# Wavelet, convolution and median kernel: one more operand of TensorE in rounded parts, x loaded again into z, and a new order of POOL's and ACT's work

## The reference

```
cA,cH,cV,cD = dwt2(x)                     # one Haar level: sums and differences of pixel pairs
proc(c)     = relu(batchnorm(einsum('bchw,oc->bohw', c, conv_w)))   # statistics over the whole batch
rimg0 = idwt2(proc(cA), proc(cH), proc(cV), proc(cD))
rimg1 = three Haar levels down and up again                          # gives x back
y = conv3x3(concat([rimg0, rimg1], channels), convW_w) + convW_b
y = relu(batchnorm(y))                                               # second batch norm
m = median of the 3x3 pixels around each pixel (zeros outside)
out = y + einsum('bchw,oc->bohw', m, L1_W) + L1_b
```

## Time and profile before

| | |
|---|---|
| median of 3 runs | 402.18 us (400.51 to 403.07) |
| profiled execution, its own time | 403.58 us |
| its span | 401.2 us |
| mean granted TensorE clock | 0.991 |
| PE busy | 383.8 us, 96% |
| DVE busy | 372.2 us, 93% |
| POOL busy | 232.5 us, 58% |
| ACT busy | 170.8 us, 43% |

### The profile page before, as it was taken

The page is one execution under the profiler, slowest core; times in us unless marked ns, Lnnn a source line. Parts: engine busy times, 40 slices in busy tenths (PEclk is TensorE's granted clock), DMA queues, the critical chain, the costliest instruction groups (busy, mean ns, idle before and its releaser), DMA issues.

```text
span 401.2 us, 3603 instructions
## 1 busy us (share of the span) xinstructions
PE 383.8 (96%) x1106; PEld 205.1 (51%) x1106; DVE 372.2 (93%) x487; ACT 170.8 (43%) x351; POOL 232.5 (58%) x213
## 2 busy tenths in 40 slices
PE   6889999999999999999999999999999999998776
PEld 2245578866454555555555545454545464443222
DVE  2889967999999999999999999999999999999994
ACT  2456674446252433333334343333424221379661
POOL 3999559460694664738474747465564740016791
PEclk9999999999999999999999999999999999999988
DMA  7980010010101001010101010101011000002665
GB/s 290 418 364 2 2 52 2 0 52 2 53 1 52 17 37 52 0 52 0 54 0 52 1 54 1 52 1 52 8 46 33 19 2 1 0 0 119 247 248 223
DMA packets 7793, 26.69 MB, mean 67 GB/s; under 512 B 992, under 2 KB 1248, under 8 KB 7776
## 3 DMA queue, kind: packets, MB, share of 16 engines
q1 hardware_dynamic: 7776, 26.48, 17.6%
HBM read 18.09 MB, written 8.39 MB: 66 GB/s over the span
## 4 chain that ended last, share of the span: by engine, by line
PE 81%; DVE 12%; POOL 3%; DMA 2%; issue 1%; SPq 0%; ACT 0%; DVEq 0%
PE conv_ps L429 60%; PE conv_ps L444 12%; PE one_ps L411 4%; PE one_ps L530 3%; DVE y L1004 2%; PE conv_ps L554 2%; DMA z<-x 2%; POOL y L241 1%; POOL y L242 1%; DVE one_ps L916 1%; DVE one_ps L925 1%; DVE sorted_cols L876 1%; DVE sorted_cols L923 1%; DVE one_ps L910 1%; DVE sorted_cols L883 1%
## 5 line engine op out<-in xcount | busy, mean ns | idle before, releaser
L429 PE MATMUL conv_ps<-ru,wt 128*128 128x512 f32 (+1 forms) x324 | 129.9, 537 | 0.0
L429 PEld LDWEIGHTS conv_ps<-ru,wt 128*128 128x128 f32 x324 | 61.3, 190 | 55.1 <-issue 52.7
L429 PE MATMUL conv_ps<-xu,wt 128*128 128x496 f32 (+3 forms) x216 | 86.6, 537 | 0.0
L663 ACT ACTIVATE y<-conv_ps,sgn 128x512 f32<-128x512 f32 (+1 forms) x36 | 24.4, 679 | 124.1 <-PE conv_ps L429 124.1
L429 PEld LDWEIGHTS conv_ps<-xu,wt 128*128 128x128 f32 x216 | 41.0, 190 | 35.6 <-issue 33.7
L248 POOL TENSOR_TENSOR ru<-z 128x512 f32<-128x512 f32 x14 | 18.2, 1301 | 59.3 <-DVE one_ps L916 59.3
L342 POOL TENSOR_TENSOR ru<-eo 128x512 f32<-128x512 f32 x16 | 17.0, 1062 | 47.5 <-DVE one_ps L874 47.4
L429 PE MATMUL conv_ps<-ru,v 128*128 128x496 f32 (+3 forms) x108 | 43.3, 537 | 0.0
L554 PE MATMUL conv_ps<-z,w 128*128 128x512 f32 x64 | 32.7, 653 | 7.4 <-POOL z L387 4.1
L411 PE MATMUL one_ps<-y,w 128*128 128x512 f32 x64 | 30.5, 601 | 5.1 <-POOL y L242 1.8
L620 ACT ACTIVATE z<-z,bn 128x256 f32<-128x256 f32 x64 | 33.1, 595 | 0.4 <-DVE bn L819 0.4
(11 more groups left out here) (141 smaller groups left out, 741.1 us busy)
## 6 DMA issues: line engine op xcount, KB each, us to landing
z<-x SPq DMA_DIRECT2D x16, 512.0 KB, 10.5
raw_place<-x SPq DMA_DIRECT2D x15, 512.0 KB, 3.2
out<-y SPq DMA_DIRECT2D x15, 512.0 KB, 2.6
wt<-w_t SPq DMA_DIRECT2D x2, 576.0 KB, 10.8
ru<-x SPq DMA_DIRECT2D x1, 512.0 KB, 14.1
out<-y SPq DMA_DIRECT2D x2, 256.0 KB, 2.6
w<-w_t SPq DMA_DIRECT2D x2, 64.0 KB, 7.9
vec<-vectors SPq DMA_DIRECT2D x1, 3.0 KB, 8.3
```

Source lines behind the costliest of these rows:

```text
L429: return nc.tensor.matmul(bank(u, b)[:, (r0 - row) * BW:(r1 - row) * BW], taps(half, kx, ky), plane[:, (r0 + dy) * BW:(r1 + dy) * BW], sta ...
L663: S.activation(at(slot(n), row * W + b, [[2, cols]]), src, ACT.Identity, scale=sgn[:, :], accum_out=y_sum[:, part:part + 1]).then_inc(y_ke ...
```

## The change

In `outputs`, the b=0 products of plane u0 for images 4 to 15 (`SPLIT0`) are done in rounded parts: `u0_hi` x `w0_hi`, `u0_hi` x `w0_lo`, then the fp32 products of ru03 as before, then `u0_lo` x `w0_hi`. ACT makes `u0_hi` and once `w0_hi`, POOL makes `u0_lo` and once `w0_lo`. u0_hi and u0_lo have no place of their own: they are the first halves of `x_hi` and `x_lo`. The second load of x goes into z (images 0 and 1: into ru03) and waits for ru12(n). POOL's eo pair goes ahead of make_lo, and u0_lo(n-1) comes after xu03(n), waiting for the new semaphore `highs_read`, which DVE's L908 gives in place of its counted step. ACT makes x_hi(n+2) behind the first half of keep_y(n), and u0_hi(n+1) after keep_p(n+2).

```diff
+    SPLIT0 = tuple(range(4, IMAGES))
...
-        raw_place = sb("raw_place", [CH, PIX])
...
+        u0_hi, u0_lo = x_hi[:, 0:HALF], x_lo[:, 0:HALF]
+        w0_hi, w0_lo = (sb(n, [CH, KY * CH], fp32r) for n in ("w0_hi", "w0_lo"))
...
         def raw(n):
-            return ru03[1] if n == 1 else raw_place
+            return ru03[n][:, :] if n < 2 else zslot(n)
...
             for n in range(IMAGES):
                 if n >= 2:
                     sp.wait_ge(raw_in[n % 2], 16 * (n // 2))
-                    sp.wait_ge(xu03_made, n if n > 2 else 1)
-                    sp.wait_ge(x_edges_made, n if n > 2 else 1)
-                sp.dma_start(raw(n)[:, :], x_img[:, n, :]).then_inc(raw_in[n % 2], 16)
+                    sp.wait_ge(ru12_made, n + 1)
+                sp.dma_start(raw(n), x_img[:, n, :]).then_inc(raw_in[n % 2], 16)
...
+            def make_u0_lo(n):
+                pool.wait_ge(highs_read, last_unit(n - 1) + 1)
+                pool.wait_ge(u0_hi_made, SPLIT0.index(n) + 1)
+                G.tensor_tensor(u0_lo, xu03[n % 2][:, 0:HALF], fl(u0_hi), ALU.subtract).then_inc(u0_lo_made, 1)
...
+            pool.wait_ge(w0_hi_made, 1)
+            G.tensor_tensor(w0_part(w0_lo), outer_left_taps(), w0_part(fl(w0_hi)), ALU.subtract).then_inc(w0_lo_made, 1)
...
                 make_ru12(G, n).then_inc(ru12_made, 1)
+                make_eo(n)
                 if n in SPLIT:
                     make_lo(n)
                 make_ru03(n)
                 make_xu03(n)
+                if n - 1 in SPLIT0:
+                    make_u0_lo(n - 1)
+            make_u0_lo(IMAGES - 1)
...
+            def u0_products(u, part, parts_taps):
+                n, row, rows = UNITS[u]
+                for ky in KY_ORDER:
+                    dy = ky - 1
+                    r0, r1 = max(row, -dy), min(row + rows, H - dy)
+                    mm = nc.tensor.matmul(bank(u, 0)[:, (r0 - row) * BW:(r1 - row) * BW], parts_taps[:, ky * CH:(ky + 1) * CH],
+                                          part[:, (r0 + dy) * BW:(r1 + dy) * BW], start=False, stop=False, skip_group_check=True)
+                return mm
...
                 for b in range(2):
-                    for ky in KY_ORDER:
-                        product(u, b, X_HALF, (0, 2)[b], planes(xu03[n % 2][:, :])[b], ky, onto=True)
+                    rounded = b == 0 and n in SPLIT0
+                    if rounded:
+                        if n == SPLIT0[0]:
+                            pe.wait_ge(w0_lo_made, 1)
+                        pe.wait_ge(u0_hi_made, SPLIT0.index(n) + 1)
+                        u0_products(u, u0_hi, w0_hi)
+                        u0_products(u, u0_hi, w0_lo)
+                    else:
+                        for ky in KY_ORDER:
+                            product(u, b, X_HALF, (0, 2)[b], planes(xu03[n % 2][:, :])[b], ky, onto=True)
                     if b == 0:
                         pe.wait_ge(ru03_made, n + 1)
                     for ky in KY_ORDER:
                         mm = product(u, b, R_HALF, (0, 2)[b], planes(ru03[n % 2][:, :])[b], ky, onto=True)
+                    if rounded:
+                        pe.wait_ge(u0_lo_made, SPLIT0.index(n) + 1)
+                        mm = u0_products(u, u0_lo, w0_hi)
                     mm.then_inc(y_done, 1)
...
             def round_x(n):
                 if n != SPLIT[0]:
-                    act.wait_ge(q_done, last_unit(SPLIT[SPLIT.index(n) - 1]) + 1)
+                    act.wait_ge(q_done, last_unit(n - 1) + 1)
+                    if n - 2 in SPLIT0:
+                        act.wait_ge(y_done, 2 * last_unit(n - 2) + 1)
...
+            S.activation(w0_part(w0_hi), outer_left_taps(), ACT.Identity).then_inc(w0_hi_made, 1)
             act.wait_ge(bn1_ready, 1)
...
                     keep_y(u, b)
+                    if b == 0 and n + 2 in SPLIT and n in SPLIT0:
+                        round_x(n + 2)
...
                 if u == last_unit(n):
+                    if n + 1 in SPLIT0:
+                        if n + 2 < IMAGES:
+                            act.wait_ge(p_done, last_unit(n + 2) + 1)
+                        else:
+                            act.wait_ge(p_done, len(UNITS))
+                        act.wait_ge(xu03_made, n + 2)
+                        act.wait_ge(x_edges_made, n + 2)
+                        S.activation(u0_hi, xu03[(n + 1) % 2][:, 0:HALF], ACT.Identity).then_inc(u0_hi_made, 1)
                     if n + 2 < IMAGES:
                         x_edges(n + 2)
                     if n + 3 < IMAGES:
                         norm_bands(n + 3)
-                if u + 2 < len(UNITS) and UNITS[u + 2][0] + 1 in SPLIT and u + 2 == last_unit(UNITS[u + 2][0]) and u > 1:
-                    round_x(UNITS[u + 2][0] + 1)
+                    if n + 3 in SPLIT and n + 1 not in SPLIT0:
+                        round_x(n + 3)
...
                 step(V.tensor_tensor(p1, pair(col_lo, 0), pair(col_lo, 1), ALU.max))
                 after(1)
-                step(V.tensor_tensor(p2, pair(col_hi, 0), pair(col_hi, 1), ALU.min))
-                after(1)
+                V.tensor_tensor(p2, pair(col_hi, 0), pair(col_hi, 1), ALU.min).then_inc(highs_read, 1)
+                after()
                 step(V.tensor_tensor(dense3, both(0), outer(col_lo), ALU.max))
-                after(1)
+                dve.wait_ge(highs_read, kept // 2)
```

More of the change, by code:

```diff
@@ L136, in wavelet_conv_median_kernel @@
         lo_taps_made = sem("lo_taps_made")
+        w0_hi_made = sem("w0_hi_made")
+        w0_lo_made = sem("w0_lo_made")
+        u0_hi_made = sem("u0_hi_made")
+        u0_lo_made = sem("u0_lo_made")
+        highs_read = sem("highs_read")
         x_hi_made = sem("x_hi_made")
@@ L214, in raw, with outer_left_taps, w0_part @@
         def raw(n):
-            return ru03[1] if n == 1 else raw_place
+            return ru03[n][:, :] if n < 2 else zslot(n)
+        def outer_left_taps():
+            return at(wt[:, :], X_HALF * KY * KX * CH, [[KX * CH, KY], [1, CH]])
+        def w0_part(t):
+            return at(t[:, :], 0, [[CH, KY], [1, CH]])
         def fl(t):
@@ L319, in make_xu03 @@
                     pool.wait_ge(y_done, 2 * (last_unit(n - 2) + 1))
-                r = raw(n)[:, :]
+                r = raw(n)
                 G.tensor_tensor(at(xu03[k][:, :], 1, [[BW, H], [1, BW - 1]]), at(r, 1, [[W, H], [2, BW - 1]]),
@@ L324, in make_xu03, with make_eo @@
                                 at(r, 0, [[W, H], [2, BW - 1]]), ALU.subtract).then_inc(xu03_made, 1)
-            def make_ru03(n):
+            even = at(eo[:, :], 0, [[UP, H], [1, BW]])
+            right = at(eo[:, :], 1, [[UP, H], [1, BW]])
+            left = at(eo[:, :], ODD, [[UP, H], [1, BW]])
+            odd = at(eo[:, :], ODD + 1, [[UP, H], [1, BW]])
+            def make_eo(n):
                 k = n % 2
@@ L329, in make_ru03 @@
                 u1, u2 = (at(ru12[k][:, :], off, [[BW, H], [1, BW]]) for off in (0, HALF))
-                even = at(eo[:, :], 0, [[UP, H], [1, BW]])
-                right = at(eo[:, :], 1, [[UP, H], [1, BW]])
-                left = at(eo[:, :], ODD, [[UP, H], [1, BW]])
-                odd = at(eo[:, :], ODD + 1, [[UP, H], [1, BW]])
                 if n > 0:
@@ L337, in make_ru03 @@
                 G.tensor_tensor(odd, u1, u2, ALU.subtract).then_inc(eo_made, 1)
+            def make_ru03(n):
+                k = n % 2
                 pool.wait_ge(eo_made, n + 1)
@@ L630, in x_edges @@
                     act.wait_ge(y_done, 2 * (last_unit(n - 2) + 1))
-                S.mul(at(xu03[k][:, :], 0, [[HALF + BW - 1, 2], [BW, H]]), at(raw(n)[:, :], 1, [[W - 3, 2], [W, H]]),
+                S.mul(at(xu03[k][:, :], 0, [[HALF + BW - 1, 2], [BW, H]]), at(raw(n), 1, [[W - 3, 2], [W, H]]),
                       -1.0).then_inc(x_edges_made, 1)
```

## The result

The changed kernel takes 403.23 us (median of 16 runs, 402.25 to 405.39) against 401.09 us of the kernel before in 16 runs beside it (400.51 to 403.76). The ratio of the means is 1.0047, interval 1.0027 to 1.0066: 1.9 us slower (1.1 to 2.6); the medians differ by 2.1. The profiled execution took 402.75, span 400.3. In this file `u0_products` is L533 and the rounded `pq` products are L476; DVE's L873, L908, L976, L925 and L1004 of before are L940, L975, L1043, L992 and L1071.

The account below looks back on a forecast made before the run. TensorE bounds the kernel at 19.22 us an image, VectorE close at 18.38. Products save 5.12; image 4 loses 2.35, the last image 5.1; the batch norm comes 0.6 later, the tail 2.2: 402.18 + 2.2 = 404.4, range 402 to 406.2.

Parts of the forecast that it names:

- Products: In outputs of images 4 to 15, rounding saves TensorE 0.465 us an image: period 18.76, 5.12 us up to outputs(14).
- Start: At the start, w0_lo adds 1.0 us to POOL, and VectorE falls back 0.95 us.
- Image 4: TensorE stalls 2.35 us for x_lo(4), now made behind the eo pair; outputs(14) ends at 337.85, 2.77 earlier.
- Blocking: VectorE steps with both inputs in SBUF and POOL's SBUF-reading steps exclude each other throughout; w0_lo costs VectorE 0.95 us.
- The last image: In outputs(15), TensorE idles 2.35 us for u0_hi and 3.25 for u0_lo: 15.2 us instead of 10.08.
- Second batch norm: Sums of squares are ready at 354.9; L925 starts at 357.3 against 356.70, 0.6 us later.
- The tail: Median 15 ends at 391.2; finish(11), mix(13) and finish(13) follow, finish(15)'s halves from 397.7, 0.9 us later at full clock.
- The 3.5 at half clock: With TensorE at half clock in the tail's mixes, the new chain of finishes and mixes ends 3.5 us later.
- I take the middle, 2.2: For the tail, the middle between 0.9 us later at full clock and 3.5 at half clock: 2.2 later.
- 410: Rival: the clock falls to 0.50 in outputs(15) around its two idles, giving 410 us; chance 0.20.
- Rival 3: u0_lo overruns L908's gap, L914 waits, VectorE's period becomes 18.98 and the bound: 408.6 us; chance 0.06.
- Rivals 2 and 4: Less lost at start, image 4 and tail: 402.1 or 400.5, chance 0.15; rounded products save nothing: 410, chance 0.03.

Follow-up runs that it names:

- experiment 4: The changed kernel without any rounded u0 products, its orders, second load and taps' parts kept: 406.17 us, ratio 1.0122 to the kernel before.
- experiment 7: The changed kernel with u0_lo made straight behind xu03, without its wait for VectorE (highs_read): 406.25 us, ratio 1.0112 to the kernel before.
- experiment 3: The changed kernel with x_lo made ahead of the eo pair for all images: 405.06 us, ratio 1.0097 to the kernel before.
- experiment 12: The changed kernel with products of zeros filling its three TensorE idles (image 4, two in outputs(15)): 403.39 us, ratio 1.0031 to the kernel before.
- experiment 5: The changed kernel with image 15 in fp32 and ten products of zeros in image 4's stall: 399.18 us, ratio 0.9936 to the kernel before.

## Why the prediction was right, and where it was not

Forecast 404.4, measured 403.23 (+2.2 against +1.9 by the means and +2.1 by the medians): the time lies in the forecast's own range. Up to the second batch norm the mechanism was right, behind it it wasn't. By its steps:

*Products.* Period 18.76 predicted, 18.74 measured; experiment 4 shows that rounding alone makes it. *Start.* VectorE and POOL late by 0.95 predicted, 0.85 and 0.75 measured. *Image 4.* Stall 2.35 predicted, 2.08 measured. outputs(14) ends at 337.58 for 337.85. *Blocking.* u0_lo in the gap behind L975 meets no two-input step, and without its wait it does (experiment 7, 0.78 an image). The rule of the Trainium skill (SBUF — State Buffer, Who interferes with whom), that such steps and POOL's exclude each other for the whole instruction, agrees with 2.68 for a step of 0.69 beside a POOL step of 2.34, and with 1.47 beside 1.30.

*The last image.* 15.2 predicted, 15.29 measured; the first idle 2.35 against 2.25. The second, 3.25, came as 1.30 of idle and 1.85 of slow work. *Second batch norm.* 354.9 against 354.66, L992 at 357.3 against 357.04.

*The tail is the step that failed, though the number held.* I let median 15 end at 391.2; it ended at 387.6. The stretched steps of before (1.01, 1.66 and 2.43 for 0.69, 3.0 us in all) were kept in my sum, though the places of the finishes that they met had moved. I hung finish(11), mix(13) and finish(13) on that end and so put the halves of finish(15) at 397.7; they came at 394.80. Against this stands a second error: I compared with the profiled execution of before, whose mixes ran at a clock of 0.50, and which is 2.2 longer than one at full clock (401.2 against 399.0). The two errors cancel in the difference, so "0.9 later at full clock" beside a measured 1.0 (43.3 against 42.3) is luck. What is late is POOL's addition and zeroing and, behind it, the last stores, of which the prediction says nothing; not finish(11).

The 3.5 at half clock did not come either. That the fall would come earlier was right where it came at all (experiments 3 and 4), but there the tail is only 0.9 and 1.3 longer than at full clock; in the profile after there is no fall. "I take the middle, 2.2" hence counted a fall that most executions don't have. Against the span of 401.2 the forecast was +2.2, and the profiled execution after came out at -0.9. What saved the number was to add the difference to the median: with 0.34 for L992 and 1.0 for the tail, 399.0 becomes 400.3, just the span after. That is 1.3 of the 2.1 between the medians; the median run is 0.5 longer than the profiled one, and the last 0.3 lies outside the span and isn't explained.

*Rivals.* The clock did fall in the last outputs, but behind the first idle, so it cost nothing (experiment 12) and 410 was far off. The Trainium skill (TensorE: Matmul & The Clock Gate, HAM oscillation) says that waits between bursts of matmuls throttle the array; the traces agree that it does (0.54 at 342 us), and show that the place decides the price: 1.4 us at image 4 (experiment 5), 1.7 behind the second idle (experiment 3), none here. It isn't certain to follow: behind experiment 3's first idle of 2.26 us the clock stayed at full. Rival 3's mechanism exists, and the added wait holds it off. Rivals 2 and 4 did not come.

What stays open: some runs of the changed kernel take 404 to 405.4 at a mean clock of 0.985 to 0.990. A fall at image 4 would explain them, and so would one in the tail as in experiments 3 and 4; none of them was traced. Why a fall follows the same stall in one execution and not in the next isn't shown either.

## What to carry to other kernels

A saving per image is kept only if the last image has the same cover: at the end of a pipeline, walk through each helper's queue once more, since what hid behind the next image's work now stands alone (here 5.2 us against 5.1 saved). Make the last image's parts as soon as their buffers are free, and give a wait that only protects the steady state (here u0_lo's for VectorE) to the steady state alone. Before a term is worked out from a profiled execution, ask whether that execution had a clock fall in that stretch: the base of the tail was off by 2.2 us for this reason. And look at the order of the last stores: one output that is late holds back all behind it.

## What the runs showed of the hardware

A single TensorE idle of 2.1 us in a stream that was otherwise full was followed, in some executions, by some 4 us at a granted clock near 0.5 (0.63 and 0.52 at image 4), in others by none (three of six profiles); ten products of zeros in the idle kept the clock at 0.998 or more in six runs of six. The slow work in the last outputs (5.74 us for 3.9) cost nothing, since TensorE's next wait was for POOL. Where a two-input step of VectorE begins just behind a POOL step, it ends after it: 2.68 us for 0.69 of work. The stores of the last four images, 512 KB each, in a row kept the DMA engines at a busy share of 0.89 to 1.03 (363 to 416 GB/s), and the last landed 3.6 us after its issue instead of 2.6.
